# Another order of the matrix products, GpSimd's additions and the copies within an iteration of attention

## The reference

```
scores = jnp.einsum('bqhd,bkd->bhqk', q, k) * scale
scores = jnp.where(causal[None, None], scores + alibi[None], NEG_INF)
probs = jax.nn.softmax(scores, axis=-1)
attn = jnp.einsum('bhqk,bkd->bqhd', probs, v).reshape(B, S, H)
```

## Time and profile before

| | us |
|---|---|
| median of three runs (lowest, highest) | 2506.91 (2504.71, 2510.05) |
| the profiled execution's own time | 2510.49 |
| its span from first to last instruction | 2508.8 |
| PE busy over the span | 2327.9 (93%) |
| DVE busy | 1634.3 (65%) |
| ACT busy | 1016.1 (41%) |
| POOL busy | 913.6 (36%) |

### The profile page before, as it was taken

How to read it: one execution, slowest core, us unless ns; L and a number is a source line. 1 busy time by engine, 2 the same in 40 slices (tenths; PEclk the granted TensorE clock), 3 DMA queues, 4 the chain that set the end, 5 groups by cost and what they waited for, 6 DMA issues and landing times. The chain is left out here.

```text
span 2508.8 us, 37558 instructions
## 1 busy us (share of the span) xinstructions
PE 2327.9 (93%) x12576; PEld 1534.6 (61%) x12576; DVE 1634.3 (65%) x4666; ACT 1016.1 (41%) x1944; POOL 913.6 (36%) x563
## 2 busy tenths in 40 slices
PE   5999999699999999999999999994899999999998
PEld 4777777454444444444444444441788888888886
DVE  5777667487677777777677677771455565556554
ACT  3222222166666666666666666663110111111110
POOL 0000000036676776766676676774011011110110
PEclk8999999879999999999999999997999999999999
DMA  5445554563323323313313313304333323333330
GB/s 202 164 163 178 190 182 149 146 195 86 73 57 85 76 56 86 82 49 86 81 49 86 81 49 86 82 15 175 108 101 97 89 83 100 100 81 92 94 100 26
DMA packets 176808, 255.85 MB, mean 102 GB/s; under 512 B 15118, under 2 KB 104846, under 8 KB 176162
## 3 DMA queue, kind: packets, MB, share of 16 engines
q1 hardware_dynamic: 176674, 254.18, 35.1%
HBM read 166.04 MB, written 87.03 MB: 101 GB/s over the span
## 5 line engine op out<-in xcount | busy, mean ns | idle before, releaser
L947 DVE CUSTOM_DVE_ANT_0 unused<-pa,distance 128x512 bf16<-128x512 f32 (+3 forms) x1536 | 776.7, 553 | 326.6 <-PE pa L784 323.2
L923 ACT ACTIVATE probs<-pa,slope 128x512 f32<-128x512 f32 (+3 forms) x1536 | 780.4, 583 | 388.8 <-PE pa L807 383.1
L763 POOL TENSOR_TENSOR probs<-probs 128x1024 f32<-128x1024 f32 (+2 forms) x256 | 679.7, 2655 | 125.9 <-ACT probs L923 109.3
L784 PE MATMUL pa<-k,ff_hi 96*128 96x512 f32 (+1 forms) x1008 | 360.6, 390 | 37.9 <-DMA slope<-in_c_slope 24.7
L821 PE MATMUL pa<-probs,v 128*32 128x512 f32 (+3 forms) x3072 | 329.0, 500 | 21.3 <-DVE att L967 13.2
L784 PEld LDWEIGHTS pa<-k,ff_hi 96*128 96x128 f32 x1008 | 192.3, 195 | 230.0 <-DVE mx L947 134.6
L1164 POOL TENSOR_TENSOR yb<-y,bias 128x1024 f32<-128x1024 f32 x32 | 77.4, 2420 | 670.0 <-DVE z L1187 631.5
L807 PE MATMUL pa<-ff_hi,k 116*128 116x512 f32 (+1 forms) x798 | 315.8, 411 | 0.0
L749 POOL TENSOR_SCALAR_AFFINE_SELECT probs<-probs 128x512 f32<-128x512 f32 x256 | 162.7, 636 | 282.5 <-ACT probs L923 280.9
L295 PE MATMUL ps<-xt_hi,wq_hi 128*128 128x512 f32 (+1 forms) x576 | 230.0, 399 | 26.5 <-DVE wq_lo L392 15.4
L1074 PE MATMUL pf<-fo_hi,at_hi 128*128 128x512 f32 x512 | 203.7, 398 | 34.5 <-DVE at_lo L1179 34.5
(11 more groups left out here) (110 smaller groups left out, 2931.3 us busy)
## 6 DMA issues: line engine op xcount, KB each, us to landing
ff_hi<-q_hi_d SPq DMA_DIRECT2D x84, 256.0 KB, 4.7
x_in<-in_L_attn_hidden_states SPq DMA_DIRECT2D x8, 2048.0 KB, 8.6
q_hi_d<-q_hi SPq DMA_DIRECT2D x64, 256.0 KB, 2.0
q_lo_d<-q_lo SPq DMA_DIRECT2D x64, 256.0 KB, 2.3
att_d<-att SPq DMA_DIRECT2D x64, 256.0 KB
at_in<-att_d SPq DMA_DIRECT2D x32, 512.0 KB, 4.3
recip<-recip_d SPq DMA_DIRECT2D x128, 128.0 KB, 5.7
x_in<-in_L_attn_hidden_states SPq DMA_DIRECT2D x32, 512.0 KB, 8.0
```

Source lines behind the costliest of these rows:

```text
L763: nc.gpsimd.tensor_tensor(o, o, probs[:, source % PR, h0:h1, 0:N], ALU.add).then_inc(add_done, 1)
L784: nc.tensor.matmul(bank[:, 0:keys], q3[u][0:3 * D, qb // BPH, h, qb % BPH * P:(qb % BPH + 1) * P], k3[u][0:3 * D, k0:k0 + keys], start=Tru ...
L923: nc.scalar.activation(probs[:, n % PR, h, 0:N], sc_ps[sc_ring.bank[use]][:, at:at + N], ACT.Exp, scale=slope[:, bass.ds(g * HPG + h, 1)]) ...
L947: nc.vector.tensor_tensor_reduce(out=unused[:, mx_ring.bank[n], 0:keys], in0=bank[:, 0:keys], in1=distance[:, d0:d0 + keys], scale=1.0, sc ...
```

## The change

The plan of an iteration is a new one. "B" is gone; each product has its own place, as V4 or O1, with a minus sign where it belongs to the iteration before. Now V6, V7, V9, V10, V11, O8 and O9 do (before: V11, O8, O9). L stands behind four maxima and all four S of step 0, T in step 9 (before: step 6). The maxima are spread otherwise: 7 5 3 1 6 5 4 5 5 3 1 3 over the steps (before: 4 4 3 3 5 5 5 5 5 3 4 2).

GpSimd makes cut 9 before cut 8, all cuts before the additions 7 to 8, and 11 to 9 before 10 to 9. In the last iteration it leaves out the additions to units 8 and 9, and TensorE takes the ones products of units 7 to 11 one by one (`TAIL`). ScalarE copies the sums of the first half after unit 8 (before: unit 6), and VectorE copies the output bank of the second half at the end of step 2 (before: step 0), the first half's at the end of step 4 as before. The waits count what is done by lists made from the plan in place of `through` and `Ring`; a values product of a unit off the diagonal and a ones product wait as before, the latter now also for the cut or the exponentials where nothing is added to its unit.

```diff
-    plan = ["S S L S M M S B M M", "S M S M S M S B M", "S M M S B M", "S M M B M", "S M S M S M S B M M",
-            "S M S M S B M S M M", "S T S M S M M B S M M", "S M S M S M B M S M", "S M S M S M B M S M",
-            "S M S M S M S B", "S M M S M B M", "S M M B"]
...
+    plan = [
+        "V6- S M M M S S M S L V7- M M M",
+        "S S S M M V9- V10- M S M M",
+        "S M O8- V11- M M S",
+        "S M",
+        "S M M O9- V0 V1 S M S M M S V2 V3 O0 M",
+        "S M M S S M S V4 M M",
+        "S S M S M M S M",
+        "S M O1 M S M S M S M",
+        "S M S M M S M S M",
+        "S V5 S M T M S M S",
+        "S M O4 S",
+        "S M M M V8",
+    ]
...
-    blocks = [[("V", 11, 1), ("O", 8, 1)], [("V", 0, 0)], [("V", 1, 0), ("O", 9, 1)], [("V", 2, 0), ("O", 0, 0)], [("V", 3, 0)],
-              [("V", 4, 0), ("O", 1, 0)], [("V", 5, 0)], [("V", 6, 0)], [("V", 7, 0)], [("V", 8, 0), ("O", 4, 0)],
-              [("V", 9, 0)], [("V", 10, 0)]]
...
-    pool_order = [("cut", 0), ("cut", 1), ("cut", 2), ("cut", 3), ("add", 2, 1, 0, 4), ("add", 3, 1, 0, 4),
-                  ("add", 5, 4, 0, 4), ("add", 6, 4, 0, 4), ("cut", 8), ("cut", 9), ("add", 7, 8, 0, 2), ("cut", 10),
-                  ("add", 7, 8, 2, 4), ("cut", 11), ("add", 10, 9, 0, 4), ("add", 11, 9, 0, 4)]
...
+    pool_order = [
+        ("cut", 0), ("cut", 1), ("cut", 2), ("cut", 3),
+        ("add", 2, 1, 0, 4), ("add", 3, 1, 0, 4), ("add", 5, 4, 0, 4), ("add", 6, 4, 0, 4),
+        ("cut", 9), ("cut", 8), ("cut", 10), ("cut", 11),
+        ("add", 7, 8, 0, 2), ("add", 7, 8, 2, 4), ("add", 11, 9, 0, 4), ("add", 10, 9, 0, 4),
+    ]
+
+    evacuate_at = {2: (1, 1), 4: (0, 0)}
+    sums_at = {2: (1, 1), 8: (0, 0)}
...
+    TAIL = ["V%d" % n for n in range(NU) if any("V%d-" % n in step for step in plan)] + ["O%d" % n for n in range(7, NU)]
+
+    def pool_steps(t):
+
+        return [x for x in pool_order if x[0] == "cut" or t < ITS - 1 or x[2] < 8]
+
+    def blocks_of(t, n):
+
+        found = [(x[0], int(x[1:].rstrip("-")), t - x.count("-")) for x in plan[n] if x[0] in "VO"]
+        return [x for x in found if x[2] >= 0]
+
+    def late_in_last(x):
+        return x[2] == ITS - 1 and x[0] == "O" and x[1] > 6
+
+    tail = [(x[0], int(x[1:]), ITS - 1) for x in TAIL]
...
+    first_maxima = [(0, x) for step in order for ahead, x in step if ahead] + [(0, ("turn", 1))]
+
+    def maxima_of(t, n):
+
+        return [(t + ahead, x) for ahead, x in order[n] if t + ahead < ITS and (t + ahead > 0)]
...
+                use = mx_use[w, item]
+                if use >= MXB:
+                    pe.wait_ge(mx_free, use - MXB + 1)
+                bank = mx_ps[use % MXB]
...
-                if n in last_add_to:
-                    pe.wait_ge(add_done, t * AD + last_add_to[n])
+                mine = [x[1] for x in block_list if x[0] == "O" and units[x[1]][0] == c and x[2] == t]
+                if (t, n) in added_to:
+                    pe.wait_ge(add_done, added_to[t, n])
+                elif n in cuts:
+                    pe.wait_ge(cut_done, t * CUTS + cuts.index(n) + 1)
+                else:
+                    pe.wait_ge(exp_done, t * EXPS + (EXPS + HPG * (n + 1)))
...
-                        elif kind == "B":
-                            some_blocks(t, n)
-                        elif kind == "L":
-                            if not first:
-                                maxima_item(t, u, ("turn", 1))
-                        elif items:
-                            maxima_item(t + 1, nu, items.pop(0))
+                        elif kind[0] in "VO":
+                            product = (kind[0], int(kind[1:].rstrip("-")), t - kind.count("-"))
+                            if product in products and not late_in_last(product):
+                                block_product(*product)
+                        elif maxima and maxima[0][1][0] == ("piece" if kind == "M" else "turn"):
+                            w, item = maxima.pop(0)
+                            maxima_item(w, w % SLOTS, item)
...
-            for n in range(NU):
-                if any(back for _, _, back in blocks[n]):
-                    for kind, m, back in blocks[n]:
-                        if back and kind == "V":
-                            values(ITS - 1, (ITS - 1) % SLOTS, m)
-                        elif back:
-                            total(ITS - 1, m)
+            for product in tail:
+                block_product(*product)
...
-                    if n == 6:
-                        take_sums(t, 0)
-                    if n == 2 and t > 0:
-                        take_sums(t - 1, 1)
+                    if n in sums_at and t >= sums_at[n][0]:
+                        take_sums(t - sums_at[n][0], sums_at[n][1])
...
-                    if n == BPH:
-                        evacuate(t, 0)
-                    if n == 0 and not first:
-                        evacuate(t - 1, 1)
+                    for w, item in maxima_of(t, n):
+                        reduce_item(w, item)
+                    if n in evacuate_at and t >= evacuate_at[n][0]:
+                        evacuate(t - evacuate_at[n][0], evacuate_at[n][1])
```

More of the change, by code:

```diff
@@ L565, in attend @@
[L565 to L578, removed]
@@ new lines, in attend @@
+    tail = [(x[0], int(x[1:]), ITS - 1) for x in TAIL]
+    block_list = [x for t in range(ITS) for n in range(NU) for x in blocks_of(t, n) if not late_in_last(x)] + tail
+    block_done = {x: p + 1 for p, x in enumerate(block_list)}
+    assert len(block_done) == len(block_list)
+    add_list = [(t, x) for t in range(ITS) for x in pool_steps(t) if x[0] == "add"]
+    add_count = {x: p + 1 for p, x in enumerate(add_list)}
+    read_by_add, added_to = {}, {}
+    for t, x in add_list:
+        read_by_add[t, x[1]] = add_count[t, x]
+        added_to[t, x[2]] = add_count[t, x]
@@ L738, in _ @@
         def _(pool):
-            for n, (count, first) in enumerate(((mx_free, MX), (exp_done, EXPS), (att_done, CREDIT),
+            for n, (count, first) in enumerate(((exp_done, EXPS), (att_done, CREDIT),
                                                 (att_stored[0], CREDIT), (att_stored[1], CREDIT))):
@@ L757, in add @@
                     pool.wait_ge(cut_done, t * CUTS + cuts.index(source) + 1)
-                before = t * AD + sum(1 for x in adds[:adds.index(("add", source, to, h0, h1))])
+                before = add_count[t, ("add", source, to, h0, h1)] - 1
                 if before:
@@ L765, in body @@
             def body(t, u, i):
-                for step in pool_order:
+                for step in pool_steps(t):
                     if step[0] == "cut":
@@ L840, in total, with block_product @@
                 last.then_inc(pv_done, 1)
-            def some_blocks(t, n):
-                for kind, m, back in blocks[n]:
[L845 to L851, removed]
+            def block_product(kind, n, t):
+                if kind == "V":
+                    values(t, t % SLOTS, n)
+                else:
+                    total(t, n)
             pe.wait_ge(consts_in, 16 * 6)
             pe.wait_ge(loaded[0], LOADS)
-            for item in flat:
+            for w, item in first_maxima:
                 maxima_item(0, 0, item)
@@ L866, in body @@
                 for n in range(NU):
-                    items = [] if last else list(order[n])
+                    maxima, products, j = maxima_of(t, n), blocks_of(t, n), 0
                     if n in (0, BPH):
                         pe.wait_ge(neg_max[u][n // BPH], (i + 1) * PUTS)
-                    j = 0
                     for kind in plan[n]:
@@ L901, in take_sums @@
             def take_sums(t, c):
-                act.wait_ge(pv_done, through("O", (1, 9)[c], t))
+                act.wait_ge(pv_done, max(block_done[x] for x in block_list if x[0] == "O" and x[2] == t and units[x[1]][0] == c))
                 act.wait_ge(att_stored[c], t * 32 + CREDIT)
@@ L963, in evacuate @@
             def evacuate(t, c):
-                dve.wait_ge(pv_done, through("V", (BPH - 1, NU - 1)[c], t))
+                dve.wait_ge(pv_done, block_done["V", (BPH - 1, NU - 1)[c], t])
                 dve.wait_ge(att_stored[c], t * 32 + CREDIT)
                 nc.vector.tensor_copy(att[:, c, :], out_ps[:, :]).then_inc(att_done, 1)
-            for item in flat:
-                reduce_item(0, None, None, item)
+            for w, item in first_maxima:
+                reduce_item(w, item)
             def body(t, u, i):
-                first, last = t == 0, t == ITS - 1
+                last = t == ITS - 1
                 for n in range(NU):
-                    if "L" in plan[n] and not first:
-                        reduce_item(t, (t - 1) % SLOTS, (t - 1) // SLOTS, ("turn", 1))
-                    if not last:
-                        for item in order[n]:
-                            reduce_item(t + 1, u, i, item)
-                    if n == BPH:
-                        evacuate(t, 0)
```

(6 more changed lines are left out.)

56 lines of the change are left out of this document (24 added, 32 removed).

## The result

The changed kernel takes 2377.43 us in the median (2376.40 to 2378.41, four runs), the one before on the same chip 2508.48 (2504.71 to 2510.13). The ratio is 0.948, interval 0.9463 to 0.9496. It gains 131 us where 108 were forecast, and ends 2.6 us under the lower end of the range.

A forecast was written before the change was run, and what follows sets the result against it. TensorE, 95% busy in the attention stage, was taken as the bound. Period 33.2 + 0.7 + 0.2 = 34.1 us; 30 x 34.1 + 36.1 = 1059.1 against 1167.3, so -108 to 2399 us; range 2380 to 2456.

The forecast's parts named there:

- Clusters (part 1): TensorE's groups of adjacent values and ones products: 0.33 us each to enter and leave; 12 become 10, saving 0.66 us.
- L (part 2): Late transpose, moved behind the next iteration's first four maxima: waits of 1.13 us ahead and 0.55 us behind go.
- rival B: VectorE's small two-input maximum held by GpSimd's addition 7 to 8; step 0's maxima 1.9 us late, 2456 us; chance 0.16.
- The copies of the output bank (part 3): Copies for V0 and V4 are done before those products come; the 0.5 us wait goes.
- the size of the floor: TensorE's sequence per iteration without any wait, added item by item: 33.9 us for the old order, 33.2 for the new.
- New waits (parts 4 and 5): 0.7 us on ScalarE's banks in steps 7 and 8; 0.2 us for GpSimd's additions 7 to 8 at the iteration's turn.
- T's move: Early transpose from step 6 to step 9: costs nothing, its row transfer landing with 0.2 to 0.9 us of cover.
- The clock: Drops to the lower clock level, 1.56 us in seven of thirty iterations, go with the waits: 11 us.
- Rival C: GpSimd's path to unit 1's exponentials is the bound: 1.5 us late in each iteration, 2444 us; chance 0.12.
- Rival D: Early transpose's row lands late, at 8 us: step 0 starts 4.6 us later, 2537 us; chance 0.06.
- Rival E: No gain: the waits at the late transpose reappear one after another, 2507 us; chance 0.04.
- The ends: First iteration gains nothing; the last falls from 41.3 to 36.1 us, a gain of 5.

The follow-up runs named there:

- a_split: Kernel after, with four pairs of neighbouring products each parted by a matmul, 14 clusters for 10: 2411.37 us, ratio 0.9613.
- b_reduce: Kernel before, with the small maximum of two SBUF tensors written as a reduction of one SBUF input: 2489.42 us, ratio 0.9924.
- a_early_l: Kernel after, with the late transpose L back as third item of step 0, V6 and V8 still ahead: 2391.97 us, ratio 0.954.
- b_late_l: Kernel before, with only the late transpose L moved, behind all four scores of step 0 and its block of products: 2510.08 us, ratio 1.0003.
- a_twice: Kernel after, with each of an iteration's two transposes issued twice into the same bank: 2378.52 us, ratio 0.9484.
- a_cut11r: Kernel after, with GpSimd's cut 11 behind both additions 7 to 8 and the small maximum as a one-input reduction: 2373.14 us, ratio 0.9458.
- a_v5: Kernel after, with product V5 moved from step 9 to step 8, between its second and third score: 2401.63 us, ratio 0.9578.
- a_cut11: Kernel after, with GpSimd's cut 11 moved behind both additions 7 to 8: 2396.74 us, ratio 0.955.
- a_o1: Kernel after, with product O1 taken earlier, in step 6, and the maxima of two steps spread around it: 2392.84 us, ratio 0.9539.

## Why the prediction came near, and what was off

**Clusters (part 1).** Right: 0.33 each was charged, a_split shows 0.32. Two fewer are 0.66 of the 3.8 us by which the period fell; the other 3.1 are waits, and the drops of the clock come on top.

**L (part 2).** Right in place and size: no wait is left at it. The reason given, cover by V8 and V6, is half of it. Of the 1.13 us ahead of L, 0.71 were VectorE held by GpSimd's addition (b_reduce), and in the new order the small maximum comes up before cut and addition and is not held; the prediction knew the hold only as rival B. The second wait (0.55) went by L's place (a_early_l). Neither L's place alone (b_late_l) nor the end of the hold alone (b_reduce) gives this: each brings up another wait.

**The copies of the output bank (part 3).** Right: in the kernel before, the score ahead of V4 has a step of 0.83, in the kernel after one of 0.33, the ordinary one ahead of a product, and there is no idle time at V0 or V4. No run moves this part alone.

**The step that failed: the size of the floor.** The prediction said: "The same sum for the old order gives 33.9, and 33.9 + 3.1 of waits is the 37.1 measured, so the sum can be trusted." The waits that it had named were 1.13 + 0.55 + 0.5 + 0.35 = 2.5; the 3.1 was what remained of 37.1, so the two sides could not disagree. The steps of the kernel before show what was left out. TensorE of the kernel before, around T (1033.65) and in step 1:

```profile
1033.68 0.47 PE L807 MATMUL pa<-q,k 116*128 116x512 f32 x1
1034.17 0.50 PE L784 MATMUL pa<-k,ff_hi 96*128 96x512 f32 x1
...
1034.78 0.33 PE L784 MATMUL pa<-k,ff_hi 96*128 96x128 f32 x1
1035.28 0.49 PE L784 MATMUL pa<-k,ff_hi 96*128 96x512 f32 x1 [0.18 <-DVE mxt_lo L960]
...
1056.07 0.39 PE L807 MATMUL pa<-ff_hi,k 116*128 116x384 f32 x1
1056.42 0.39 PE L784 MATMUL pa<-k,ff_hi 96*128 96x256 f32 x1
```

Behind T two steps take 0.49 and 0.50 where 0.23 and 0.06 are ordinary; with their neighbours some 0.9 us are lost there, where 0.35 was named. In step 1 the scores of 384 columns take 0.35 to 0.41 where 0.18 to 0.28 is ordinary, with the maxima between them some 0.7 us, where nothing was named.

The other side of the same error is the price list. In the profile after the two transposes do not take 0.38 each: the step from L is 0.20, that from T 0.03, and the 0.09 more at the maximum behind T may be a wait. Kernel after, TensorE around T:

```profile
1026.74 0.23 PE L811 MATMUL pa<-k,ff_hi 96*128 96x128 f32 x1
1026.81 0.27 PE L821 MATMUL pa<-ident,mx 128*16 128x128 f32 x1
1026.84 0.48 PE L811 MATMUL pa<-k,ff_hi 96*128 96x512 f32 x1
1027.15 0.34 PE L834 MATMUL pa<-ff_hi,k 116*128 116x384 f32 x1
```

That is about 0.5 too much. A maximum of 128 columns was charged 0.14 and takes 0.06 and some 0.05 behind it, eight times: 0.25 too much. With crumbs at V1, V10 and V11 the floor is some 0.9 lower, 32.3 for the new order and 33.0 for the old. The old order's waits were then 4.1 us, not 3.1, which the places above bear out (1.13 + 0.55 + 0.5 + 0.9 + 0.7 = 3.8, and small ones). The new order's waits are 1.0 where 0.9 were forecast (below). A floor 0.9 lower and waits 0.1 higher give 0.8; the period missed by 0.74 (34.1 less 33.36), 22 us in thirty. These prices are read from the starts; the transposes' is supported by a_twice (0.11 each), that of the narrow maxima was not tested.

**New waits (parts 4 and 5).** Well sized. In TensorE's rows of steps 7 and 8, kernel after, the idle time that the prediction named as a sign does not stand, but some score matmuls have a step of 0.34 where 0.24 is ordinary. TensorE's rows, and the weight load of the second such score:

```profile
1022.78 0.50 PE L834 MATMUL pa<-ff_hi,k 116*128 116x512 f32 x1
1023.12 0.40 PE L811 MATMUL pa<-k,ff_hi 96*128 96x512 f32 x1
1023.36 0.50 PE L834 MATMUL pa<-ff_hi,k 116*128 116x512 f32 x1
1023.70 0.57 PE L811 MATMUL pa<-k,ff_hi 96*128 96x384 f32 x2
```

```profile
1023.36 0.19 PEld L834 LDWEIGHTS pa<-ff_hi,k 116*128 116x128 f32 x1 [0.28 <-ACT probs L944]
```

The weight load at 1023.36 has waited for ScalarE and starts together with its matmul, where that of the maximum at 1023.12 started 0.23 ahead of it. From 1022.78 to 1023.12 and from 1023.36 to 1023.70 are two of six such places (S6d, S7a, S7c, S8a, S8b and the maximum M39); by medians they are 0.55 us together (forecast 0.7). The waits that go back to the additions 7 to 8, at M9 and S1d, are 0.25 (forecast 0.2; a_cut11r recovers them, and makes the period 33.04). Around T lie another 0.2. The prediction took T's move to cost nothing and looked only at the transfer; the transfer is in time (no idle time ahead of V6), and a_v5 shows VectorE as the one that is late there.

**The clock.** Right: all drops are gone. b_reduce adds that the wait at L need not vanish with everything else for that; its decrease from 0.86 of idle time to at most 0.2 was enough, and gave 11 us with the rest of the order as it was. In b_late_l, with idle times of 0.27, 0.32 and 0.62 within 3.3 us (the rows shown), three drops of seven are left.

**Rival B** did not occur, by 0.65 us, and a_cut11 shows that it was real. Its price was too high, 0.8 for 1.9 in an iteration: only one maximum is late, since all it needs is that VectorE has read the shortest one (a reading of the rows, not tested). The Trainium skill (GPSIMD Engine Reference, "Specifications") names VectorE instructions with two SBUF inputs among those that contend for GpSimd's SBUF interface; 2125 ns with two inputs and 188 with one at the same place agree.

**Rival C** did not occur: the waits at M9 and S1d are 0.26, not 1.5. **Rival D** did not either: there is no idle time ahead of V6. (Its turning point is a landing of 7.0 us rather than 6.8: 8 less the 1.0 between 38.7 and 37.7.) Rival E is what the move of L does alone (b_late_l), not what the parts do together.

**The ends.** The last iteration takes 37.2 for 36.1. The second iteration starts 1.0 later, behind 2.02 of idle time where 0.84 stood. The 3.6 us less in `finish` were not forecast. No run was made to explain these three; they stay open; they partly cancel (+1.0, +0.9, -3.6) and make up the other 1.8 us of the miss.

## What to carry to other kernels

A price list that is added up over a sequence must be checked where nothing waits, item by item against the gaps between starts; to take the waits as what is left proves nothing, and makes their removal look too cheap. When TensorE shows no idle time any more, a move of one item still moves its waits to another engine's slack: the three edits of the new order that were made singly and meant to gain (a_cut11, a_o1, a_v5) lost 15 to 24 us, and the one gain, 4 us, came with VectorE freed of GpSimd first. And an experiment that changes nothing in the time may be two effects that cancel (b_late_l, a_twice): compare the steps, not only the totals. Where a VectorE instruction with two SBUF inputs can come up while GpSimd runs, write it with one input.

## What the runs showed of the hardware that was not expected

- A VectorE instruction of 16 columns with both inputs in SBUF ends only with the GpSimd instruction that runs beside it: 905 and 2125 ns when it begins under an addition, 174 to 177 ns when it begins 0.05 us ahead of a cut. As a reduction of one input it takes 186 to 190 ns in the same places.
- The clock's drops in one iteration of four, 1.56 us each, ended when the idle time at one place fell from 0.86 us to 0.2 or less (b_reduce), while waits of up to 0.4 and 0.5 us elsewhere stayed. With L moved alone and a longest wait of 0.62 us (b_late_l) they came in three iterations of thirty. The kernel a_cut11 has a single idle time of 0.62 in an iteration, and its clock stays at 1.00.
- A second transpose directly behind the first moves the next matmul by 0.11 us; waits behind it absorb that, and the kernel's time grows by 1 us in 2377 (a_twice).
- A wait that ends just in time shows no idle time on TensorE but makes the step of a 512-column matmul 0.34 where 0.24 is ordinary. Its own weight load then starts within 0.01 us of it instead of 0.1 to 0.23 ahead. The first matmul behind a values or ones product shows the same two numbers, which is one part (0.11) of a cluster's 0.33.
